# A two-layer graph network: the last group in tiles, the last round written out, the two layers' ends reordered

## The reference, cut to what matters

```python
# 6250 nodes of 256 values, 200000 edges sorted by dst, edge features of 128 values
# layer 0
msg = relu(x[src] + (edge_attr @ W_edge + b_edge))
agg = segment_sum(msg, dst)
h = relu(((1 + eps) * x + agg) @ W1 + b1) @ W2 + b2
h = relu((h - mean(h, axis=0)) * rsqrt(var(h, axis=0) + 1e-5) * gamma + beta)
x = layernorm(x + h)
# layer 1: attention with 4 heads of 64
z = einsum('nd,hdf->nhf', x, W)
e = leaky_relu(es[src] + ed[dst], 0.01)          # es, ed: z times the two halves of att
ex = exp(e - segment_max(e, dst)[dst])
x = layernorm(x + segment_sum(ex / segment_sum(ex, dst)[dst] * z[src], dst))
```

## Time and profile before

| | us |
|---|---|
| time, median of 3 runs | 4116.05 (4114.78 to 4118.70) |
| the profiled execution's own time | 4123.64 |
| its span, first to last instruction | 4121.5 |
| GpSimd busy in the span | 3030.0 (74%) |
| TensorE busy | 3058.7 (74%) |
| VectorE busy | 2329.3 (57%) |
| ScalarE busy | 787.0 (19%) |
| mean granted clock of TensorE | 0.880 |

### The profile page before, as it was taken

One profiled execution on the slowest core, in us unless ns is written; L12 is line 12 of the kernel. 1 busy time (PEld: TensorE's weight loads), 2 busy tenths in 40 slices (PEclk: granted clock), 3 DMA queues, 4 the chain that ended last, 5 costly groups with the idle time before them and its releaser, 6 DMA issues.

```text
span 4121.5 us, 55537 instructions
## 1 busy us (share of the span) xinstructions
PE 3058.7 (74%) x13497; PEld 2358.1 (57%) x13597; DVE 2329.3 (57%) x5849; ACT 787.0 (19%) x1504; POOL 3030.0 (74%) x3229
## 2 busy tenths in 40 slices
PE   6888888888888888889866666666666666566665
PEld 5666666676667666767644444444544445454554
DVE  5444444444444444444456666676776777776776
ACT  2222222222222222222330000010110111111212
POOL 7777777777777777777457777777777777777775
PEclk9999999999999999999987787878778777877777
DMA  5555555555555555555365555555555555555554
GB/s 178 157 159 156 156 155 159 165 154 157 153 165 159 158 161 157 165 155 161 90 169 158 162 158 157 158 166 158 162 161 158 166 162 162 162 162 166 161 167 115
DMA packets 321250, 650.02 MB, mean 158 GB/s; under 512 B 149807, under 2 KB 170521, under 8 KB 321209
## 3 DMA queue, kind: packets, MB, share of 16 engines
q0 software_dynamic: 150272, 413.00, 35.3%
q1 hardware_dynamic: 164448, 230.16, 18.3%
q10 hardware_dynamic: 6489, 6.40, 0.5%
HBM read 636.22 MB, written 13.08 MB: 158 GB/s over the span
## 4 chain that ended last, share of the span: by engine, by line
POOL 23%; PE 23%; issue 17%; DMA 16%; DVE 9%; DVEq 8%; ACT 3%; ACTq 1%; POOLq 0%; SPq 0%
POOL rows L390 23%; PE psum L889 8%; DMA rows<-in_x,idx 8%; PE psum L878 8%; DMA rows<-z_tab,idx 7%; DVEq L755 4%; DVE rows L1013 3%; PE psum L875 2%; PE psum L898 1%; PE psum L917 1%; DVEq L751 1%; PE psum L608 1%; ACT agg_sb L967 1%; DVE hot_t L746 1%; DVE rows L825 1%
## 5 line engine op out<-in xcount | busy, mean ns | idle before, releaser
L390 POOL DMA_INDIRECT rows<-in_x,idx x1568 | 1496.8, 955 | 501.1 <-issue 446.9
L390 POOL DMA_INDIRECT rows<-z_tab,idx x1568 | 1496.6, 954 | 483.4 <-issue 451.1
L1013 DVE TENSOR_TENSOR rows<-rows,psum 128x1024 f32<-128x1024 f32 x392 | 478.5, 1221 | 1089.2 <-DMA rows<-in_x,idx 775.1
L608 PE MATMUL psum<-rows,onehot 128*128 128x260 f32 x3136 | 1060.9, 511 | 40.9 <-issue 40.7
L608 PEld LDWEIGHTS psum<-rows,onehot 128*128 128x128 f32 x3136 | 806.7, 264 | 226.4 <-issue 49.0
L878 PE MATMUL psum<-weights,edge_room 128*128 128x256 f32 x3136 | 814.2, 382 | 5.6 <-issue 0.4
L889 PE MATMUL psum<-rows,onehot 128*128 128x256 f32 x3136 | 761.4, 387 | 0.0
L963 ACT ACTIVATE rows<-rows 128x1024 f32<-128x1024 f32 x392 | 414.3, 1057 | 1479.3 <-DVE rows L1013 1479.3
L878 PEld LDWEIGHTS psum<-weights,edge_room 128*128 128x128 f32 x3136 | 604.1, 193 | 159.1 <-issue 5.9
L889 PEld LDWEIGHTS psum<-rows,onehot 128*128 128x128 f32 x3136 | 592.4, 194 | 75.1
L825 DVE TENSOR_TENSOR rows<-rows,psum 128x1024 f32<-128x1024 f32 x392 | 460.7, 1216 | 77.9 <-ACT psum L697 77.9
(11 more groups left out here) (149 smaller groups left out, 1655.8 us busy)
## 6 DMA issues: line engine op xcount, KB each, us to landing
dst_t<-in_dst_jp SPq DMA_DIRECT2D x197, 512.0 KB
edge_room<-in_edge_t SPq DMA_DIRECT2D x196, 512.0 KB, 3.9
rows<-in_x,idx POOLq DMA_INDIRECT x1568
rows<-z_tab,idx POOLq DMA_INDIRECT x1568
z_tab<-edge_room SPq DMA_DIRECT2D x14, 455.0 KB, 6.9
idx<-in_src_idx SPq DMA_DIRECT2D x392, 4.0 KB, 1.7
dst_t<-in_x_t SPq DMA_DIRECT2D x14, 448.0 KB, 5.7
rows<-in_x_t SPq DMA_DIRECT2D x14, 448.0 KB, 6.1
```

The source lines that it names most:

```text
L390: nc.gpsimd.indirect_dma_start(rows[0:count, u, j, 0:width], None, table, bass.IndirectOffsetOnAxis(ap=idx[0:count, u, j:j + 1], axis=0)). ...
L608: last = pe.matmul(agg_ps[0:WIN, 0:width], onehot[:, hot, j, :], rows[:, u, j, 0:width], start=(j == 0), stop=(j == J - 1))
L1013: dve.tensor_tensor(half, half, psum[:, 2 * b:2 * b + 2, :].rearrange("p b (j d) -> p (b j) d", j=2), ALU.add).then_inc(added, 1)
```

## The change

The last group lies tile by tile: edge e of the group is in partition e mod 128 of column e // 128, so three columns hold its 320 edges (128, 128 and 64), and three gathers fetch them. On all engines `rounds` ends its loops after round 47 and writes round 48 out (PEELED = 1), so that the last group can be treated apart: in layer 0 its second half is left out (edge products, addition, relu, sum) and three one-hot tiles are made instead of eight; in layer 1 one half is scaled, three columns are summed, and nothing is prepared for a 197th group.

At the end of layer 0 TensorE's second product of chunk 12 moves behind all turns, the second product signals each half of its output, and VectorE's statistics move. At the end of layer 1 the x part of chunk 13 (copy, turns, normalisation) moves ahead of the last group's sum, TensorE turns the sums and denominators of chunk 13 straight from where they are summed, without ScalarE's two copies, and of the output's four tiles ScalarE scales and stores two, while VectorE scales and SP stores the other two.

```diff
@@ constants
+LAST = EDGES - (GROUPS - 1) * GROUP
+PEELED = 1
@@ rounds(): every engine's last round is written out; the loops end one round earlier
+            def last_rounds():
+                for n in range(ROUNDS - PEELED, ROUNDS):
+                    for u in range(RING):
+                        body(n, u, n * RING + u)
...
             lo = end(chunks)
-            with eng.If(lo < ROUNDS - 1):
-                until(lo, ROUNDS - 1)
+            with eng.If(lo < ROUNDS - 1 - PEELED):
+                until(lo, ROUNDS - 1 - PEELED)
+            last_rounds()
             return chunks
@@ the last group's tiles
-        def filled(g):
-            return -(-(EDGES - (GROUPS - 1) * GROUP) // J) if isinstance(g, int) and g == GROUPS - 1 else P
+        def landed(rounds_before, g):
+            return 16 * J * rounds_before + 16 * tiles(g)
+        def last_group(g):
+            return isinstance(g, int) and g == GROUPS - 1
+        def tiles(g):
+            return -(-LAST // P) if last_group(g) else J
+        def last_outputs(eng, first_part, rest, last, c0):
+            with eng.If(c0 < CHUNKS - 1):
+                with eng.Fori(c0, CHUNKS - 1) as c:
+                    rest(c)
+                    first_part(c + 1)
+            last(CHUNKS - 1)
@@ SP in layer 1
-            if fast and layer == 1:
-                load_ends(ROUNDS, 0, GROUPS)
+            if layer == 1:
+                lo = (CHUNKS - 1) * CHUNK
+                sp.wait_ge(f_half, 1)
+                sp.dma_start(t["out"][lo + 2 * SUB:lo + 3 * SUB, :], out_c[0:SUB, 2, :]).then_inc(f_out, 16)
+                sp.dma_start(t["out"][lo + 3 * SUB:NODES, :], out_c[0:TAIL - 3 * SUB, 3, :]).then_inc(f_out, 16)
@@ gather
-        def gather(L, table, width, u, count=P):
-            for j in range(J):
+        def gather(L, table, width, u, g=0):
+            for j in range(tiles(g)):
+                count = min(P, LAST - j * P) if last_group(g) else P
@@ PE, output of layer 1: x_part and rest are the two halves of finish_nodes; new is
+            def last(c):
+                pe.wait_ge(layer1.group_done, GROUPS)
+                at = slice(c * CHUNK, (c + 1) * CHUNK)
+                turn_dens(den[:, at])
+                turn_tiles(acc[:, :, at], 2)
@@ ACT, output of layer 1 (deviation, scale, store are pieces of finish_nodes)
+            def last(c):
+                deviation(c)
+                scale(range(2))
+                store(c, 2)
@@ DVE, output of layer 1 (x_part and normalise are the halves of finish_nodes)
+            def last(c):
+                normalise(c)
+                for s in range(2, TILES):
+                    dve.tensor_scalar(out_c[0:SUB, s, :], out_c[0:SUB, s, :], fin_r[0:SUB, s:s + 1],
+                                      fin_m[0:SUB, s:s + 1], ALU.mult, ALU.add)
+                dve.drain().then_inc(f_half, 1)
@@ pass_matmuls, layer 1 (pass_act and pass_vector alike)
-                if fast and layer == 1:
+                if fast and layer == 1 and not last_group(g):
                     spread_ed(i, u + 1, g + 1)
...
+            if layer == 1:
+                x_part(c0 if fast else 0)
             sum_first(RING - 1, GROUPS - 1)
             turn_first(GROUPS - 1, False)
-            last_nodes(pe, finish_nodes, c0 if fast else 0)
+                last_outputs(pe, x_part, rest, last_part, c0 if fast else 0)
@@ pass_vector, layer 1
-                    for q in range(2):
+                    for q in range(1 if fast and last_group(g) else 2):
...
-                if fast and layer == 1:
+                if fast and layer == 1 and not last_group(g):
                     make_hot_t(i, u + 1, g + 1)
@@ single0_matmuls
-                edge_products(i, u, g, 1).then_inc(half_done, 1)
+                if not last_group(g):
+                    edge_products(i, u, g, 1).then_inc(half_done, 1)
@@ second_product: one signal for each half of the output
-                last.then_inc(a_pe2, 1)
+                    last.then_inc(a_pe2, 1)
@@ end of single0_matmuls
-            pe.wait_ge(added, 2 * GROUPS - 1)
-            with pe.If(c0 > 0):
-                second_product(c0 - 1)
             turn_window(u(GROUPS - 3), GROUPS - 3, False)
             sum_half(u(GROUPS - 2), GROUPS - 2, 1, False).then_inc(half_done, 1)
             sum_half(u(GROUPS - 1), GROUPS - 1, 0, False).then_inc(half_done, 1)
-            turn_window(u(GROUPS - 2), GROUPS - 2, False)
-            sum_half(u(GROUPS - 1), GROUPS - 1, 1, False).then_inc(half_done, 1)
+            turn_window(u(GROUPS - 2), GROUPS - 2, False).then_inc(half_done, 1)
             turn_window(u(GROUPS - 1), GROUPS - 1, False).then_inc(half_done, 1)
-            pe.wait_ge(added, 2 * GROUPS)
+            pe.wait_ge(added, 2 * GROUPS - 1)
+            with pe.If(c0 > 0):
+                second_product(c0 - 1)
             last_nodes(pe, finish_last, c0)
@@ single0_act: second_bias
-                act.wait_ge(a_pe2, c + 1)
                 for k in range(HALF):
+                    act.wait_ge(a_pe2, 2 * c + k + 2)
@@ end of single0_vector
-            add_window((GROUPS - 3) % RING, GROUPS - 3, 2 * GROUPS + 1)
-            add_window((GROUPS - 2) % RING, GROUPS - 2, 2 * GROUPS + 3)
+            add_window((GROUPS - 3) % RING, GROUPS - 3, 2 * GROUPS)
             earlier_statistics(c0, 2)
-            earlier_statistics(c0, 1)
-            add_window((GROUPS - 1) % RING, GROUPS - 1, 2 * GROUPS + 4)
+            add_window((GROUPS - 2) % RING, GROUPS - 2, 2 * GROUPS + 2)
+            add_window((GROUPS - 1) % RING, GROUPS - 1, 2 * GROUPS + 3)
             last_nodes(dve, finish_last, c0)
+            dve.wait_ge(a_act2, CHUNKS + 1)
+            statistics(CHUNKS - 1, TAIL)
@@ inputs: edge e of the last group lies at partition e % P of tile e // P
+    def placed(a):
+        a = a.reshape(GROUPS, P, J, *a.shape[1:])
+        last = a[-1:].reshape(1, J, P, *a.shape[3:]).swapaxes(1, 2)
+        return np.concatenate([a[:-1], last])
```

More of the change, by code:

```diff
@@ L289, in build, with rounds @@
         m_out = sem("m_out")
-        f_copied, f_den, f_turn, f_mv, f_std, f_r, f_nrm, f_out, f_xt = (
-            sem(f"f_{x}") for x in ("copied", "den", "turn", "mv", "std", "r", "nrm", "out", "xt"))
+        f_copied, f_den, f_turn, f_mv, f_std, f_r, f_nrm, f_out, f_xt, f_half = (
+            sem(f"f_{x}") for x in ("copied", "den", "turn", "mv", "std", "r", "nrm", "out", "xt", "half"))
         block = ctx.enter_context(nc.Block())
-        def rounds(eng, body, finish_nodes=None, ends=0, begun=False, peeled=0):
+        def rounds(eng, body, finish_nodes=None, ends=0, begun=False):
             def until(lo, hi):
@@ L316, in rounds @@
             if finish_nodes is None:
[L317 to L320, removed]
+                until(0, ROUNDS - 1 - PEELED)
+                last_rounds()
                 return
@@ L491, in turn_tiles, with turn_dens, x_part @@
                     last.then_inc(f_xt, 1)
-            def finish_nodes(c, done):
+            def turn_dens(x):
+                pe.sem_inc(passed, 1)
+                for s in range(TILES):
+                    last = pe.transpose(turn_ps[0:SUB, s * HEADS:(s + 1) * HEADS], x[:, s * SUB:(s + 1) * SUB],
+                                        ident[0:HEADS, 0:HEADS])
+                last.then_inc(f_den, 1)
+            def x_part(c):
                 pe.wait_ge(f_copied, 3 * c + 1)
@@ L496, in finish_nodes, with rest @@
                 turn_tiles(x_c, 6)
+            def rest(c):
                 pe.wait_ge(f_copied, 3 * c + 2)
[L498 to L502, removed]
+                turn_dens(den_c)
                 pe.wait_ge(f_copied, 3 * c + 3)
@@ L887, in sum_half @@
                 pe.wait_ge(layer0.msg_ready, 2 * g + b + 1)
-                for j in range(4 * b, 4 * b + 4):
+                for j in range(4 * b, min(4 * b + 4, end)):
                     last = pe.matmul(banks[4 + u % 2][:, 0:D], onehot[:, u % 2, j, :], rows[:, u, j, 0:D],
-                                     start=(j == 0), stop=(j == J - 1))
+                                     start=(j == 0), stop=(j == end - 1))
                 return last
@@ L972, in body @@
                     copy_window((u - 2) % RING, g - 2, 2 * g + 1)
-                relu(u, g, 1)
+                if not last_group(g):
+                    relu(u, g, 1)
             def first_relu(c):
@@ L1050, in earlier_statistics @@
             def earlier_statistics(c, back):
+                if isinstance(c, int):
+                    dve.wait_ge(a_act2, c + 2 - back)
+                    statistics(c - back, CHUNK)
+                    return
                 with dve.If(c > back - 1):
```

165 lines of the change are left out of this document (107 added, 58 removed).

## The result

The changed kernel takes 4135.51 us (median of 6 runs, 4130.6 to 4137.31), the one before 4115.95 in the same series (6 runs): ratio 1.0046 [1.0033, 1.0059]. It is 19.6 us slower; forecast were 15.1 us less. The two profiled executions differ by less, 13.0 us of span: the one before took 7.6 us more than the median of its first three runs, the one after 0.9 more than its median.

A forecast was written before the change was run, and what follows sets the result against it. GpSimd's issue pace was taken to bound both passes, so only the layers' ends could gain: 10.5 + 5.45 - 0.8 = 15.1 us, from 4116.05 to 4101.0 us. Range 4097 to 4109; the forecast's own, at chance 0.60, 4098.5 to 4103.5.

The forecast's parts named there:

- the first one: Both layers' passes run at GpSimd's issue pace, and the change touches nothing in the 195 full groups.
- five gathers fewer: Last group, each layer: 5 x 1.25 us of GpSimd's time, costed at nothing because other engines end last.
- The jump over the loop: Engines jump over the loop's code to the written-out round: 0.4 us lost per layer, other end 2.4.
- The sign that I named: Forecast is wrong if idle time marked issue of over 2 us stands behind the next-to-last chunk's finish.
- Rival 2: Jump over the loop is distant, 2.65 us where 0.61 is counted: 4105 to 4106 us, chance 0.14.
- Layer 0's end: Reordered turns and second product, faster first product and bias by halves gain 7.2 + 2.7 + 0.6 = 10.5 us.
- the last turn: End of layer 0, TensorE: turn of group 195 at about 2008.6 instead of 2014.60, 6.0 us earlier.
- the first product: End of layer 0, chunk 13: starts 7.2 us earlier and takes 3.02 us instead of 5.68.
- rival 1: TensorE's clock stays low at the end of layer 0: 4103.6 to 4106.5 us, chance 0.12.
- Layer 1's end: Earlier division (4.4 us) and output in two queues (1.05 us) gain 5.45 us before the jump's 0.4.
- Division: End of layer 1, VectorE: starts about 1.9 us after the last addition, 4.4 us earlier than before.
- Rival 4: Grown program makes layer 1's backward loop jumps fetch, up to 2.65 us a round: 4135 us, chance 0.10.

The follow-up runs named there:

- r9_three_d: r2_peel with the last group fetched by three gathers (128, 128, 64 rows): 4148.19 us, ratio 1.0072; as r9_three on a slow chip 5411.25 us, 0.9992.
- r2_peel: The kernel before with only the last round written out, on all engines: 4127.71 us, ratio 1.0013.
- r7_gap: r2_peel without TensorE's layer 0 code for rounds between the last finished chunk and the last round: 4123.37 us, ratio 1.0005.
- r10_behind_d: The kernel after, TensorE's skipped layer 0 code put behind the layer's end: 4130.80 us, ratio 1.0031; as r10_behind on a slow chip 5388.73 us, 0.9949.
- r1_same: The kernel before with nothing changed but one unused name, the control: 4122.61 us, ratio 1.0001.
- r4: The kernel before with about 500, 170, 460 and 60 never-reached instructions more on TensorE, ScalarE, VectorE and SyncE: 4121.41 us, ratio 1.0000.
- r5: The kernel before with a never-reached output store on SyncE, moving x in the list of DRAM tensors: 4122.48 us, ratio 0.9986.
- r3_sizes: The kernel after with the destination table and node_at at their old sizes, one group and one column more: 4144.05 us, ratio 1.0050.
- r8_full: The kernel after with eight gathers of 128 rows each for the last group: 5403.23 us on a slow chip, ratio 0.9986.
- r6: The kernel after with the two last output stores issued by ScalarE instead of SyncE, moving x back in the tensor list: 4137.88 us, ratio 1.0041.

## Why the prediction was wrong

**The step that failed is the first one:** "So both passes run at the pace at which GpSimd issues, and the reader should see that nothing in the change touches the 195 full groups." The pace itself was touched. Writing the last group's gathers as three (128, 128 and 64 rows) instead of eight of 40 rows made the gathers of layer 0 15 ns dearer on average: r9_three_d shows it with this edit alone. It is worth 24 us against r2_peel by the ratios and 18.5 by the two profiles, and 20.5 us in the two long pieces of the profile after. All six profiles of kernels with the eight gathers of 40 rows have a first gather of 1145 to 1148 ns and a median of 946 to 949 in layer 0; all fourteen of the others have 1116 to 1119 and 957 to 960. I costed five gathers fewer at nothing and had no case in which GpSimd's own price changes, though the bound was GpSimd by my own reading.

**The jump over the loop** was a term of the sum and mis-sized: 0.4 us in layer 0, with 2.4 kept as the other end. It is 5.3 us in r2_peel (5.7 against r7_gap) and 7.8 in the kernel after (60.62 against r10's 52.86). The sign that I named, idle time of over 2 us marked issue behind the next-to-last finish, came true with 5.04. Rival 2 had the mechanism and took its price from a jump of VectorE's. Two things were missed: behind the longer pause TensorE's clock is at 0.50, and the jump falls where TensorE is behind already, so that GpSimd waits 4.02 us for it. In layer 1 no cost shows; the 0.4 I took there is smaller than what such pieces differ by from profile to profile.

**Layer 0's end** was right once the jump is away: forecast were 6.0 us for the last turn, 7.2 for the first product and 10.5 in all; r10_behind_d shows 5.9, 7.2 and 10.05. The first product takes 3.27 us for 3.02 forecast and 5.68, at a granted clock of 1.00, so rival 1 didn't come about there:

```profile
2034.58:2037.80 3.22, 3.22 (x8) 1.43 (x8) 1.15 (x2) 1.27 (x2) 0.00 (x0) 1.00 0.00 0
```

(the kernel after). VectorE's idle time at the batch norm is 3.74 us where it was 2.65, but it is 3.33 to 3.69 in three profiles without the change as well (r1, r4, r5).

**Layer 1's end** was about right: 5.05 forecast with the jump, 5.2 measured in the kernel after, 4.5 and 3.7 in r3_sizes and r10_behind_d against the same profile before. The division, the normalised x and the last stores after:

```profile
4119.38 1.91 DVE L601 TENSOR_SCALAR psum<-psum,fin_ln 112x256 f32<-112x256 f32 x4 [0.22 <-PE psum L516]
4121.87 0.42 DVE L826 TENSOR_TENSOR acc<-acc,psum 128x256 f32 x1 [0.58 <-PE psum L444]
4123.73 1.29 DVE L614 TENSOR_TENSOR onehot<-psum,fin_den 112x512 f32<-112x512 f32 x2 [0.18 <-PE psum L516]
4129.12 1.09 ACT L563 ACTIVATE onehot<-onehot,fin_m,fin_r 112x256 f32<-112x256 f32 x2 [0.51 <-DVEq L633]
4129.18 0.74 DVE L638 TENSOR_SCALAR onehot<-onehot,fin_r,fin_m 112x256 f32<-112x256 f32 x2
out<-onehot SPq DMA_DIRECT2D x1, 90.0 KB, 3.1
```

Division 1.86 us after the addition (1.9 forecast; 4.04 before), and 5.4 us from the start of scaling to the end (5.4).

**Rival 4** had the right sign and a time next to the measured one (4135), by a mechanism that didn't happen, so that was luck. In r7_gap the program has grown ahead of layer 1's loops too, and the piece from the batch norm to chunk 12's finish in layer 1 takes 2034.15 us there, 2034.49 before (2036.59 in r2_peel, against some 17 us more that this rival had for a layer).

**What the sum doesn't hold.** The forecast carried the profiled execution's 7.6 us over the median along unchanged. Profile to profile the loss is 13.0 us, median to median 19.6; the other 6.6 are what single executions differ from their series, and the pieces don't show where they lie.

**What stays open.** Which property of GpSimd's program sets the price. The rows of the last group's gathers are the nearest candidate: r8_full has eight gathers and the old counts to wait for, and still the median and the first gather of the kernels with three, so what it shares with r9_three is only that the eight gathers of 40 rows are gone. That isn't shown as the cause: r8_full never ran on a chip of the first kind, its other engines have the kernel after's programs, and no run changes the rows alone. Why the first gather gets shorter (1.15 to 1.12 us) while the ordinary ones get longer isn't explained. And no run shows the kernel that would join both repairs, r10_behind with the old eight gathers of 40 rows.

## What to carry to other kernels

Where one engine's pace is the bound, first look in the profile after at the mean of its one instruction, before any chain: 15 ns on 1563 gathers outweighed the 7.5 us won at both ends. An edit of that engine's program, even in a place that runs once, is to be timed by itself. And a block that is normally skipped should stand behind the path that is taken: on the engine that is late, the jump over it took 7.8 us of the 10 that the new end of layer 0 brings without it.

## What the runs showed of the hardware

- The price of a gather depends on what GpSimd's program has in another place: on chips of the first kind 954 to 957 ns in layer 0 with eight gathers of 40 rows for the last group (before, r2, r4, r5, r7; 960 in the slowest execution of r1_same), 969 to 973 with three of 128, 128 and 64 (the kernel after, r3, r6, r9_three_d, r10_behind_d), the same rows and tables for the 195 others.
- A jump of TensorE over four groups' code: 5.03 us of pause instead of 1.10, and eight sums at 3.21 us instead of 1.73 behind it (r2_peel, r7_gap); in the kernel after, the clock granted behind such a pause is 0.50.
- The kernel before takes 4116 to 4124 us in some series and 5357 to 5421 in others, far more than any edit here moves it. Each series was one chip at one time, so the runs don't tell the chip from what else went on. In the latter the change, with the skipped code moved, is 0.3 to 0.5% faster than before (r10_behind).
